# A selective scan in which five of 24 delta*u tiles are fanned out by TensorE from eight rows, and the y stores are issued by ScalarE

## The reference, cut to what matters

```python
def step(state, inp):
    d, b, c, uu = inp
    dA = jnp.exp(d[..., None] * A_neg[:, None, :, :])
    state = dA * state + (d * uu)[..., None] * b[:, :, None, :]
    y = jnp.einsum('kbcn,kbn->kbc', state, c)
    return (state, y)
init = jnp.zeros((K, B, C, N), jnp.float32)
_, ys = jax.lax.scan(step, init, (d_t, B_t, C_t, u_t))
```

## Time and profile before

| | us |
|---|---|
| median of 3 runs (17228.62 to 17241.57) | 17231.57 |
| the profiled execution, its own time | 17236.15 |
| its span, first to last instruction | 17234.5 |
| first to last scan of layer 2 | 8540.1 to 15593.3 |

### The profile page before, as it was taken

One profiled execution on the slowest core, in us unless ns is written; L12 is line 12 of the kernel. 1 busy time (PEld: TensorE's weight loads), 2 busy tenths in 40 slices (PEclk: granted clock), 3 DMA queues, 4 the chain that ended last, 5 costly groups with the idle time before them and its releaser, 6 DMA issues. The chain is left out here.

```text
span 17234.5 us, 361490 instructions
## 1 busy us (share of the span) xinstructions
PE 12704.4 (74%) x127392; PEld 8742.7 (51%) x127392; DVE 11266.0 (65%) x10439; ACT 7765.1 (45%) x13769; POOL 6782.0 (39%) x3199
## 2 busy tenths in 40 slices
PE   7889999888999954454466666666666666667799
PEld 5666666666666632222244444444444444444477
DVE  5666666666666655555477777777777777775532
ACT  4444444444444434544455545554555545552200
POOL 1000000000000014423577777887778877772100
PEclk9999999999999977777677777777777777776799
DMA  5222222222222237766899999999999999998711
GB/s 124 65 57 58 59 59 53 66 56 66 59 59 59 53 106 186 179 153 159 209 233 233 234 230 233 235 235 234 236 232 235 237 228 232 233 230 222 197 39 40
DMA packets 2038805, 2633.89 MB, mean 153 GB/s; under 512 B 1083612, under 2 KB 1935324, under 8 KB 2013404
## 3 DMA queue, kind: packets, MB, share of 16 engines
q1 hardware_dynamic: 1991388, 2487.10, 59.5%
q0 software_dynamic: 12288, 86.71, 2.3%
q10 hardware_dynamic: 34944, 57.81, 1.2%
HBM read 2103.61 MB, written 556.32 MB: 154 GB/s over the span
## 5 line engine op out<-in xcount | busy, mean ns | idle before, releaser
L1731 DVE TENSOR_TENSOR_SCAN L2.h<-L2.ps,L2.db 128x912 f32<-128x912 f32 x2688 | 5515.0, 2056 | 1569.2 <-POOL L2.db L1587 1522.1
L1587 POOL TENSOR_TENSOR L2.db<-L2.du,L2.bt 128x896 f32<-128x896 f32 x2688 | 5580.1, 2096 | 1551.7 <-DMA L2.du<-du 1468.0
L1608 PE MATMUL L2.ps<-L2.dm,L2.wa 32*128 32x112 f32 x21504 | 2306.9, 346 | 2471.1 <-DVE L2.h L1731 2343.4
L1669 ACT ACTIVATE L2.ps<-L2.ps 128x896 f32<-128x896 f32 x2688 | 2424.5, 902 | 3503.4 <-PE L2.ps L1608 3501.6
L1608 PEld LDWEIGHTS L2.ps<-L2.dm,L2.wa 32*128 32x128 f32 x21504 | 1899.6, 246 | 3268.2 <-DVE L2.h L1731 2940.3
L1621 PE MATMUL L2.ps<-L2.h,L2.cd 128*8 128x96 f32 x50176 | 2575.6, 362 | 5.5 <-DVE L2.h L1731 5.5
L1621 PEld LDWEIGHTS L2.ps<-L2.h,L2.cd 128*8 128x8 f32 x50176 | 1439.4, 108 | 583.6 <-DVE L2.h L1731 5.6
L314 POOL TENSOR_TENSOR L1.x_res<-L1.x_res,L1.ob 96x3136 f32 (+1 forms) x16 | 95.4, 5977 | 2582.2 <-ACT L1.qv L457 2582.2
L314 POOL TENSOR_TENSOR L0.x_res<-L0.x_res,L0.ob 96x3136 f32 (+1 forms) x16 | 95.9, 6007 | 2367.8 <-ACT L0.qv L457 2367.8
L366 PE MATMUL L1.p_proj<-L1.xt,L1.w_hi 128*96 128x448 f32 x3024 | 826.4, 383 | 194.2 <-DVE L1.xt L560 167.5
L366 PE MATMUL L0.p_proj<-L0.xt,L0.w_hi 128*96 128x448 f32 x3024 | 826.3, 383 | 194.3 <-DVE L0.xt L560 167.6
(11 more groups left out here) (255 smaller groups left out, 19811.4 us busy)
## 6 DMA issues: line engine op xcount, KB each, us to landing
L2.du<-du SPq DMA_DIRECT2D x5376, 224.0 KB, 6.6
L2.dm<-d SPq DMA_DIRECT2D x896, 336.0 KB, 6.8
y<-L2.ysum SPq DMA_DIRECT2D x896, 84.0 KB
L0.left<-table SPq DMA_DIRECT2D x48, 1176.0 KB
L0.right<-table SPq DMA_DIRECT2D x48, 1176.0 KB
L1.left<-table SPq DMA_DIRECT2D x48, 1176.0 KB
L1.right<-table SPq DMA_DIRECT2D x48, 1176.0 KB
du<-L2p.work SPq DMA_DIRECT2D x64, 784.0 KB, 7.5
```

The lines of the kernel that those rows point to most:

```text
L1587: pool.tensor_tensor(db[:, n % RB, :, 2:ROW], du[:, n % RD, :].rearrange("p (c t) -> p c t", t=SPAN), row, ALU.mult)\
L1608: mm = pe.matmul(decays[n % RA][:, lo:lo + SPAN], wa[rows, u * QUAD + e, :], dm[rows, u * QUAD + e, :], start=True, stop=True)
L1669: act.activation(a, a, ACT.Exp).then_inc(a_ready, 1)
L1731: dve.tensor_tensor_scan(h[:, half, u * UNIT:(u + 1) * UNIT, :].rearrange("p c t -> p (c t)"), decays[n % RA], db[:, n % RB, :, :].rearran ...
```

## The change

Units n = 5, 9, 13, 17 and 21 of each span no longer load 128 rows of `du`. Instead:

- SP's `load_few` loads the eight rows of each of the two parts (g) of such a unit, 14 KB each, into `few`: part 0 to partitions 0 to 7, part 1 to 32 to 39. Unit n = 4i+5 is loaded when SP is at n = 4i.
- ACT's `make_hi` rounds `few` to fp32r (`few_hi`), and DVE's `make_lo` subtracts it from `few` for the remainder (`few_lo`), both on 40 x 448, in front of unit 4i on their engine.
- PE's `fan_out` multiplies the 0/1 matrix `fan` by the two, which puts each of the eight rows on its 16 partitions of PSUM bank 7 (128 x 448): part 0 behind unit 4i+2, part 1 behind unit 4i+4, and behind the fill there, if there is one.
- ACT's `copy_du` copies bank 7 to `du`: part 0 in front of unit 4i+3, part 1 in front of unit 4i+4. POOL waits for both copies instead of a load.

Since bank 7 is taken, the fills of y have only bank 6: `sum_states` waits until the fill before has been copied. ACT does `take_sum` now in front of `decay` and `carry` of a unit, not behind. `ysum` is one buffer, and `store_y` is issued by ACT at the end of each half, behind unit 11; the first `take_sum` of the next half waits until those stores have landed.

```diff
+        def by_pe(n):
+            return n > 1 and n % 4 == 1
+        FANS = 2 * UNITS // 4 - 1
...
+            def load_few(k, s, i):
+                n = 4 * i + 5
+                before = count(sp, k, s, FANS, max(i - 1, 0))
...
+                    sp.wait_ge(lo_made, before)
...
+                    sp.dma_start(few[32 * g:32 * g + BATCH, i % 2, :], rows).then_inc(few_in[i % 2], 16)
...
-                    load_du(k, s, half, u)
-                    if u == 2 and earlier is not None:
-                        sp.wait_ge(sum_out, fills + (2 - FILLS))
-                        steady(sp)
-                        store_y(*earlier, half)
+                    n = half * UNITS + u
+                    if n % 4 == 0 and n // 4 < FANS:
+                        load_few(k, s, n // 4)
+                    if not by_pe(n):
+                        load_du(k, s, half, u)
...
+            def fan_out(i, g, k, s):
+                copies = count(pe, k, s, 2 * FANS, 2 * i + g)
+                if g == 0:
+                    pe.wait_ge(lo_made, count(pe, k, s, FANS, i + 1))
+                if not (isinstance(copies, int) and copies == 0):
+                    pe.wait_ge(du_copied, copies)
+                rows = slice(32 * g, 32 * g + BATCH)
+                pe.matmul(ps[:, 7, 0:QUAD * SPAN], fan[rows, :], few_hi[rows, :], start=True, stop=False)
+                pe.matmul(ps[:, 7, 0:QUAD * SPAN], fan[rows, :], few_lo[rows, :], start=False, stop=True)\
+                    .then_inc(fanned, 1)
...
-                bank = 6 + (half * FILLS + f) % 2
-                pe.wait_ge(sum_out, fills + (f + 1))
+                pe.wait_ge(sum_out, fills + (f + 2))
...
                         sum_states(1 - half, f, before)
+                    n = half * UNITS + u
+                    if n % 4 == 2 and n // 4 < FANS:
+                        fan_out(n // 4, 0, k, s)
+                    if n % 4 == 0 and n:
+                        fan_out(n // 4 - 1, 1, k, s)
...
+            def copy_du(i, g, units, copies):
+                n = 4 * i + 5
+                act.wait_ge(fanned, copies + (2 * i + g + 1))
+                act.wait_ge(b_ready, units + (n + 1))
+                act.copy(du[:, n % RD, g * QUAD * SPAN:(g + 1) * QUAD * SPAN], ps[:, 7, 0:QUAD * SPAN]).then_inc(du_copied, 1)
...
                 for u in range(UNITS):
-                    decay(half * UNITS + u, spreads)
-                    carry(half, u, units, begun)
                     f = u - FIRST_FILL - 1
                     if 0 <= f < FILLS and not first:
                         if f == 0:
-                            act.wait_ge(y_stored[1 - half], count(act, k, s, 64, 64 * half))
+                            act.wait_ge(y_stored[half], count(act, k, s, 64, 64))
                         take_sum(k - 1 if begun and half == 0 else k, 1 - half, f, before)
+                    n = half * UNITS + u
+                    if n % 4 == 3 and n // 4 < FANS:
+                        copy_du(n // 4, 0, units, copies)
+                    if n % 4 == 0 and n:
+                        copy_du(n // 4 - 1, 1, units, copies)
+                    if n % 4 == 0 and n // 4 < FANS:
+                        make_hi(n // 4, k, s)
+                    decay(n, spreads)
+                    carry(half, u, units, begun)
+                if not first:
+                    act.wait_ge(sum_out, before + (FILLS + 2))
+                    steady(act)
+                    if half:
+                        store_y(k, s, 0)
...
                 if half == 0:
                     make_cd(k, s, before)
```

More of the change, by code:

```diff
@@ L1410, in scan_layer @@
         HALVES = 2 * NSPANS
+        FEW = 32 + BATCH
         h = m.sb("h", [128, 2, HALF, ROW])
@@ L1454, in count @@
             return eng.snap(s * scale + (k * NSPANS * scale + add))
+        def by_pe(n):
+            return n > 1 and n % 4 == 1
+        FANS = 2 * UNITS // 4 - 1
+        moved = [[n for n in range(2 * UNITS) if n % RD == q and not by_pe(n)] for q in range(RD)]
         def span_of(s):
@@ L1499, in load_du, with half_span @@
                     sp.dma_start(du[:, slot, g * QUAD * SPAN:(g + 1) * QUAD * SPAN], src).then_inc(du_in[slot], 16)
-            def store_y(k, s, half):
-                for q in range(4):
-                    at = s * SPAN + SPAN // 4 * q
-                    if k % 2:
-                        at = at * -1 + (TOK - SPAN // 4)
-                    rows = slice(at, at + SPAN // 4) if isinstance(s, int) else bass.ds(at, SPAN // 4)
-                    place = y_dram[k, :, rows, half * HALF:(half + 1) * HALF]
-                    sp.dma_start(place, ysum[32 * q:32 * q + BATCH, half, :, :]).then_inc(y_stored[half], 16)
-            def half_span(k, s, half, earlier, later, table):
+            def half_span(k, s, half, later, table):
                 units = count(sp, k, s, 2 * UNITS, half * UNITS)
-                fills = count(sp, k, s, 2 * FILLS, half * FILLS)
                 for u in range(UNITS):
@@ L1566, in _ @@
             for half in range(2):
-                sp.wait_ge(sum_out, (DIRS * HALVES - 1 + half) * FILLS + 2)
-                store_y(DIRS - 1, NSPANS - 1, half)
-            for half in range(2):
                 sp.wait_ge(y_stored[half], 64 * DIRS * NSPANS + 64)
@@ L1578, in span @@
                 units = count(pool, k, s, 2 * UNITS)
-                loads = count(pool, k, s, 32 * 2 * UNITS // RD)
+                loads = {q: count(pool, k, s, 32 * len(moved[q])) for q in range(RD) if moved[q]}
+                copies = count(pool, k, s, 2 * FANS)
                 for half in range(2):
@@ L1655, in _, with store_y @@
             act.wait_ge(cleared, 1)
-            act.wait_ge(image_in, 16)
+            act.wait_ge(image_in, 32)
+            def store_y(k, s, half):
+                for q in range(4):
+                    at = s * SPAN + SPAN // 4 * q
+                    if k % 2:
+                        at = at * -1 + (TOK - SPAN // 4)
+                    rows = slice(at, at + SPAN // 4) if isinstance(s, int) else bass.ds(at, SPAN // 4)
+                    place = y_dram[k, :, rows, half * HALF:(half + 1) * HALF]
+                    act.dma_start(place, ysum[32 * q:32 * q + BATCH, :, :]).then_inc(y_stored[half], 16)
             def make_cd(k, s, fills):
@@ L1676, in carry, with make_hi @@
                 act.copy(db[:, n % RB, :, 1], src).then_inc(carried, 1)
+            def copy_du(i, g, units, copies):
[3 more added lines that the diff above has]
+                act.copy(du[:, n % RD, g * QUAD * SPAN:(g + 1) * QUAD * SPAN], ps[:, 7, 0:QUAD * SPAN]).then_inc(du_copied, 1)
+            def make_hi(i, k, s):
+                act.wait_ge(few_in[i % 2], count(act, k, s, 32 * len(range(i % 2, FANS, 2)), 32 * (i // 2 + 1)))
+                if not (isinstance(s, int) and k == 0 and s == 0 and i == 0):
+                    act.wait_ge(fanned, count(act, k, s, 2 * FANS, 2 * i))
+                act.copy(few_hi[:], few[:, i % 2, :]).then_inc(hi_made, 1)
             def take_sum(k, half, f, fills):
@@ L1717, in _, with make_lo @@
             dve.memset(zero[:], 0.0)
+            dve.memset(few[:], 0.0)
             dve.memset(ps[:], 0.0).then_inc(cleared, 1)
+            dve.wait_ge(image_in, 32)
+            dve.tensor_copy(fan[:], fan_raw[:]).then_inc(fan_made, 1)
+            def make_lo(i, k, s):
+                dve.wait_ge(hi_made, count(dve, k, s, FANS, i + 1))
+                if not (isinstance(s, int) and k == 0 and s == 0 and i == 0):
+                    dve.wait_ge(fanned, count(dve, k, s, 2 * FANS, 2 * i))
+                dve.tensor_tensor(few_lo[:], few[:, i % 2, :], few_hi[:].bitcast(F32), ALU.subtract).then_inc(lo_made, 1)
             def span(k, s):
```

55 lines of the change are left out of this document (43 added, 12 removed).

## The result

| | us |
|---|---|
| before, median of 4 runs (17228.62 to 17241.57) | 17234.71 |
| with the change, median of 4 runs (17888.08 to 17912.97) | 17899.07 |
| ratio, 95% interval | 1.0392 (1.0379 to 1.0405) |
| forecast, range | 17,610; 17,050 to 17,950 |

The account below looks back on a forecast made before the run. Loads of `du` bound the kernel at 63.0 us a span; afterwards 49.2 of scans plus gaps 1.75, 3.4, 5.2, 1.75, 2.95 and 2.0 make 66.3. Times 112 spans that is +370, with +10 once: 17,610 us, range 17,050 to 17,950.

Parts of the forecast that it names:

- Loads no longer the bound: In the scan of layer 2: POOL's idle time for loads of `du` falls to little, DMA share about 0.80.
- The floor of 53.6 us a span for the loads: DMA loads: 63.0 us a span scaled from 14,112 to 12,012 KB at the same rate, 9.4 us less.
- rival 3: The stalls vanish and loads bind at 53.6 us a span: 16,180 us, or 16,700 at half; chance 0.08.
- `make_lo` costed at nothing: DVE's subtraction, 0.52 us, runs between ACT's rounding and the exponential's end while DVE waits anyway: nothing added.
- The chain of PE and ACT: Fills, products, fan-outs and copies delay exponentials: gaps of 1.75 and 3.4 (units 4, 8), 1.75 and 2.95 (units 16, 20).
- y's issue: ACT at each half's end: four stores take 4.2 us, in gaps of 5.2 (unit 12) and 2.0 us (unit 0).
- The scans: DVE's scans with nothing late: four in 8.18 us, 49.2 us a span of 24 units.
- Cheap issue on ACT: y's four stores take 1.5 us to issue on ACT, so 61.6 us a span and 17,090 us; chance 0.14.
- The chain does not bite: All forecast stalls vanish and loads bind at 53.6 us a span: 16,180 us, half of that gain 16,700; chance 0.08.
- Late stores: ACT's `take_sum` at u = 4 waits for y's stores to land; 17,890 us if landing takes 14 us; chance 0.18.

Follow-up runs that it names:

- e9: e8 with y's stores issued by SP at its unit 2, one `ysum`, instead of by ACT: 16885.41 us, 0.9803 of before.
- e1: The changed kernel without the remainder `few_lo`, its subtraction on DVE and its product on PE: 17489.07 us, 1.015 of before.
- e11: The changed kernel with the remainder's subtraction on POOL instead of DVE, nothing left out: 17712.31 us, 1.0276 of before.
- e8: e4 with the fp32 fan-outs one unit earlier on PE, y still on ACT's queue: 16748.93 us, 0.9722 of before.
- e2: The changed kernel with y's stores back on SP's queue, still one `ysum`: 17378.39 us, 1.0087 of before.
- e3: The changed kernel without fan-outs, all 24 units loaded; y on ACT, one `ysum`, one bank: 17048.12 us, 0.9891 of before.
- e6: e4 with ACT's copy of the second part behind its unit's exponential and carry, and y on SP: 17195.35 us, 0.9975 of before.
- e12: e8 with y's four stores and ACT's `cd` copies spread over units instead of standing between the halves: 16838.87 us, 0.9773 of before.
- e4: The changed kernel with each fan-out one fp32 product of the loaded rows, no rounding or remainder: 17719.12 us, 1.0284 of before.
- e7: The kernel before with only y's stores moved to ACT's queue; two `ysum`, two banks, no fan-out: 17097.77 us, 0.9928 of before.

## Why the prediction was right in direction and short in size

- **Loads no longer the bound: right.** POOL's wait for `du` fell to 10.0 us, the DMA share to 0.76 (0.80 forecast). First to last scan took 7696.6 us against about 7420.
- **The floor of 53.6 us a span for the loads: never reached, and doubtful.** It scales bytes at the old rate. In e9, with those bytes, POOL waits for loads again at 59.75 us a span, because SP's stream of issues is full (70.7 us of waiting in 6000). It was nearly as full in the kernel before (62.6). The forecast did not rest on this floor; its rival 3 did.
- **`make_lo` costed at nothing: the step that failed.** "It runs between ACT's rounding and the exponential's end ... while DVE waits anyway: nothing." Its own work was sized well: 0.48 us behind POOL's end against 0.52. But it first waits for the product that POOL is in, and that had begun 0.42 us before it, because the same copy of bank 7 lets POOL go. So it takes 2.13 us in front of units 4, 8, 12 and 16, and ends 1.3 us behind the exponential's carry. This is the excess at units 4 and 16: 3.45 and 3.52 against 1.75; e1 and e11 without it on DVE show 1.94 and 1.86 at unit 4. With its product on PE the remainder costs 410 us (e1), more than the 289 missed. It also lengthens the next product on POOL by 0.4.
- **The chain of PE and ACT: right in place and nearly in size.** Without the subtraction (e1), the gaps of units 4, 8, 16 and 20 are 1.94, 2.86, 2.18 and 2.36 against the forecast's 1.75, 3.4, 1.75 and 2.95, 9.3 in all against 9.85 (the forecast had both products of a fan-out, e1 has one). So the direction was no luck: without the remainder the kernel is still 1.5% slower than before. e8 shows from the other side that the fan-out's place made them.
- **y's issue: right in size and in place.** 4.39 us against 4.2, and the end of half 0 was 5.86 against 5.2 (4.71 without the subtraction). At the end of half 1 it is 2.10 without the subtraction, against the forecast's 2.0. e2 takes the stores away and keeps 1.81 there, but that is the subtraction, which the forecast had at nothing.
- **The scans: a small gain not foreseen, and some luck.** Four follow in 7.88 us, where it was 8.18; over a span the scans with their normal hand-overs take 68.75 less the six gaps of 21.4, 47.3 us against 49.2. The gaps were 4.4 over the forecast's 17.05 and this gave 1.9 back; hence 68.75 against 66.3, 2.45 x 112 = 274 of the 289 us missed. Without this gain and the 0.8 us that unit 20 came out under its forecast, errors that run the other way, the time would have passed the upper end of the range.
- **The rivals.** Cheap issue on ACT: refuted by the 4.39. The chain does not bite: refuted by the changed kernel, though e8 came to 16,749, near its half-way 16,700, by a change of order. Late stores: 46.0 us in 6000, not here. But its mechanism is real, and held ACT for 633.7 to 879.2 us in e3, e6 and e12, where loads or issue times stood otherwise.

The net of the parts, from the runs: moving y and sharing bank and buffer gains 187 us (e3), and the fan-outs on top of it lose 851 (17899 less 17048), though they take 15% of the bytes.

## What to carry to other kernels

An instruction that is put "where its engine waits anyway" must also be checked against what the other engines run at that moment: here DVE's 0.5 us became 2.1 at four of its five places, since the event that released it also started POOL. Where an operand moves from a load to a chain over three in-order engines, try each link a unit earlier than it is needed; on PE this was worth more here (970 us, e4 to e8) than either change of the arithmetic (410 in e1, 180 in e4). When loads are late, ask too what the engine that issues them waits for: in e9 it waited for almost nothing, and 15% fewer bytes left the loads late. And an issue time, a landing time and a buffer's reuse are one sum: e6, e9 and e12 each took away one and paid at another.

## What the runs showed of the hardware that was not expected

- A 40x448 instruction on DVE whose sources and output are all in SBUF ended 0.48 us (two sources) or 0.25 us (one, in the median) behind the end of the POOL product under way, in some 550 of 560 cases each; DVE shows as busy in the meantime, so the busy share of 4929.72 in 6000 us hides some 1.4 us of waiting each time, in the mean. The POOL product behind it took 2.48 and 2.25 us where others take 2.10.
- The same four stores of 84 KB issued on ACT's queue instead of SP's raised the rate of all transfers from 233 to 239 GB/s with the same bytes (e7). The Trainium skill, "DMA: Bandwidth & Descriptors", Issuing engines are not separate DMA queues, says that several issuing engines save only sequencer time; the trace agrees, since SP waited 62.6 us for free slots with the stores in its stream and 1387.3 without them. That the stores were also issued at another moment was not told apart from this.
- Of four stores in a row on ACT's queue the first two take 0.28 us each to issue, and all four 4.44 in the changed kernel and 2.99 in e7 (medians). Issued apart (e12) each takes 0.28, and no gap was left at the ends of the halves.
- A scan takes 2.02 us in the median with the change and 2.06 before and in e11, with the same operands. In e1, e4 and e8 both values occur, in shares near one half. The cause is open.
